# Filler products of two attentions moved to half as many places, two at a place

## The chip, the cores and the metric

One core of one Trainium2 chip runs the whole kernel. The metric is the device time of one launch in microseconds (us). Three runs of the kernel before took 2307.36, 2316.95 and 2318.63 us, median 2316.95 us. The profile is of one further execution.

## The reference, cut to what matters

The input is x of 8 sequences of 512 rows of 256 numbers. Each sequence goes through two blocks, both with 16 heads of 16 columns:

```python
x = x + layernorm(attention_1(layernorm(x)))      # causal, 250 keys back, rotary positions
x = x + layernorm(ffn(layernorm(x)))
# ffn(src):
sa  = attention_2(src)                            # full 512 x 512, rotary positions
x   = rmsnorm(src + sa)
shared = swiglu(x @ W_shared_in) @ W_shared_out   # 256 -> 2*512, then 512 -> 256
h      = swiglu(x @ W1_shared)                    # 256 -> 2*512
w      = gates of the best 2 of 8 experts in the better of 2 groups
routed = sum over e of (h @ W2_experts[e]) * w[:, e]   # 512 -> 256, eight times
out    = rmsnorm(x + shared + routed)
```

All experts are computed for all rows and weighted afterwards, so the amount of matrix work does not depend on the data.

## The kernel before, in words

Everything is computed transposed or straight as TensorE (PE) wants it, in tiles of 128 rows; a sequence is four such tiles. A pass of the outer loop (`batch`, eight passes) does both attentions of sequence i, and beside them the feed-forward part of sequence i-1, and the final norms of sequence i-2. Pass 0 has no feed-forward part to do; after the last pass the part of sequence 7 is done alone.

Each attention (`attention(i, f, e, a)`, a = 0 for the first and 1 for the second) is one list of steps, m from -28 to 63, and every engine walks the same list in its own order of instructions. There are 64 units (a head and a 128-row tile each, in four groups of four heads, 16 units to a group). At a step:

- `max_unit` (L644): for unit m+28, while there is one (that is for m up to 35), PE multiplies queries by keys into one of two PSUM banks (four banks for units 12 to 23). VectorE (DVE) takes the row maximum of it: L1008 with the mask for the first attention, L1011 for the second. The product for unit u waits until the maximum of unit u-2 (u-4 with four banks) has been taken.
- `score_unit` (L670): for unit m, from m = 0 on, PE computes the transposed scores with the maximum folded in; ScalarE (ACT) takes the exponential (L535), GpSimd (POOL) masks it in the first attention (L438, L442). The unit waits for the exponential of two units (later four units) before.
- `weigh` (L684): four times in a group PE multiplies four units' probabilities by the values; `max_rows` (L652) and `outputs` (L696) are four small transposes each, once in a group.
- Fillers: matrix products of the feed-forward part, which have nothing to do with this attention, stand at places given by two lists. `HIDDEN_AT` (32 entries, first attention) holds the up projections: entry s is one product of 128x128 by 128x512 in full fp32 (L710, `hidden`), which the trace shows as two instructions. Four entries make one block of hidden columns: two for the gated half into bank fb0, two for the other half into fb1. After the second of them ACT takes tanh (`ACT_LAG` = 1 step later), DVE the two elementwise products (`gated_half` and `hidden`, L1177 and L1184, `DVE_LAG` = 2 steps later); the next block's first product of a half waits for the DVE step that read that bank. `OUT_AT` (28 entries, second attention) holds the expert products: an entry is three products of 128x128 by 128x512 in fp32r (L732, `expert_out`), four entries make one output tile, which DVE adds to the sum with two instructions (L1199).

The order on PE within a step is: max unit, score unit, weigh and outputs where due, row transposes, then the filler. The two lists are worked out as

```python
QUIET = [g * UNITS + n for g in range(NGR) for n in (2, 5, 8, 12)]
QUIET_OUT = [g * UNITS + n for g in range(NGR) for n in (2, 8, 12)]
HIDDEN_AT = spread(8 * NH - len(QUIET), 10 - LEAD, -1) + QUIET
OUT_AT = spread(len(OUT_BESIDE) * NH - len(QUIET_OUT), 1 - LEAD, -1) + QUIET_OUT
```

With NGR = 4, UNITS = 16, NH = 4, LEAD = 28, the places of the up projections are -18 to -11, -9 to -3, -1, and then 2, 5, 8, 12, 18, 21, 24, 28, 34, 37, 40, 44, 50, 53, 56, 60. Those of the expert products are -27, -26, -24, -22, -21, -19, -17, -15, -14, -12, -10, -8, -7, -5, -3, -1, and then 2, 8, 12, 18, 24, 28, 34, 40, 44, 50, 56, 60.

The steps before m = 0 are called the lead below, those from 0 to 35 the body (max and score units), those from 36 on the tail (score units alone).

Of the kernel before, what the change touches and what calls it, by code (L numbers as in the profile page):

```python
# [22 lines left out]
NH = HID // P  # L23
# [5 lines left out]
NGR = H // GH  # L29
UNITS = GH * NT  # L30
# [5 lines left out]
LEAD = 28  # L36
# [3 lines left out]
def spread(steps, first, last):  # L40
    return [first + s * (last - first) // (steps - 1) for s in range(steps)]
# [2 lines left out]
LAST_STACKS_AT = 6 - LEAD  # L44
ROWS_FROM, LOGITS_AT = 2 - LEAD, 7 - LEAD

QUIET = [g * UNITS + n for g in range(NGR) for n in (2, 5, 8, 12)]
QUIET_OUT = [g * UNITS + n for g in range(NGR) for n in (2, 8, 12)]
HIDDEN_AT = spread(8 * NH - len(QUIET), 10 - LEAD, -1) + QUIET
OUT_FIRST, OUT_BESIDE = range(2, 7), range(9, 16)  # L50
OUT_END = {0: (((0, 0), (0, 1)), ((0, 2), (0, 3)), ((1, 0), (1, 1), (1, 2), (1, 3))),
           1: (((16, 0), (16, 1)), ((16, 2), (16, 3)), ())}
OUT_HEADS = {0: ((17,), (), (18,), (19,), ()), 1: ((), (7,), (), (8,), ())}
OUT_AT = spread(len(OUT_BESIDE) * NH - len(QUIET_OUT), 1 - LEAD, -1) + QUIET_OUT
ACT_LAG, DVE_LAG, HIGH_LAG = 1, 2, 3
GATES_FROM = LOGITS_AT + 2
GATE_EXPS_AT = (GATES_FROM + 6, GATES_FROM + 12)
# [11 lines left out]
def build(nc, x, in_w, out_w, wq, wkc, wvc, wk, wv, wo, w_si, w_so, w1, w2, wgg, weg,  # L69
# [3 lines left out]
    with ctx:  # L73
# [302 lines left out]
        def _(pool):  # L376
# [47 lines left out]
            def hidden_low(f, n):  # L424
                pool.wait_ge(s_hh, f * N_HH + n + 1)
                g.tensor_tensor(h_r[:, 1, n, :], sg[:, n % 2, :], h_r[:, 0, n, :].bitcast(F32),
                                ALU.subtract).then_inc(s_hl, 1)

            def mask_probs(i, f):

                for m in range(0, ALL, 2):
# [13 lines left out]
                    if f is not None:  # L445
                        for k in range(NH):
                            if min(HIDDEN_AT[4 * (NH + k) + 3] + HIGH_LAG, ALL - 1) // 2 * 2 == m:
                                hidden_low(f, k)
# [20 lines left out]
        def _(act):  # L469
# [37 lines left out]
            def tanh(f, n):  # L507
                act.wait_ge(s_up, f * N_UP + n + 1)
                if n >= 1:
                    act.wait_ge(s_sg, f * N_SG + n)  # L510
                nc.scalar.activation(th[:, :], fb[0][:, :], ACT.Tanh, scale=0.5).then_inc(s_th, 1)  # L511

            def hidden_high(f, n):
                act.wait_ge(s_ht, f * N_HT + n + 1)
                copy(h_r[:, 0, n - NH, :], sg[:, n % 2, :]).then_inc(s_hh, 1)
# [6 lines left out]
            def attention(i, f, a):  # L522
                for m in range(-LEAD, ALL):
# [15 lines left out]
                    if f is not None and a == 0:  # L539
# [4 lines left out]
                        for n in range(2 * NH):  # L544
                            if HIDDEN_AT[4 * n + 1] + ACT_LAG == m:
                                tanh(f, n)
                            if n >= NH and min(HIDDEN_AT[4 * n + 3] + HIGH_LAG, ALL - 1) == m:
                                hidden_high(f, n)
# [52 lines left out]
        def _(pe):  # L601
# [97 lines left out]
            def hidden(f, s):  # L699

                n, half, c = s // 4, s // 2 % 2, s % 2
                u, m = n // NH, n % NH
                if s == 0:
                    pe.wait_ge(s_gr, f + 1)
                elif n >= 1 and c == 0 and half == 0:
                    pe.wait_ge(s_sg, f * N_SG + n)
                elif n >= 1 and c == 0 and half == 1:
                    pe.wait_ge(s_ht, f * N_HT + n)
                col = half * HID + m * P
                product = mm(fb[half][:, :], wup_s[:, u, c, col:col + P], xn_t[:, c, :], start=(c == 0), stop=(c == NC - 1))  # L710
                if c == NC - 1:
                    product.then_inc((s_up, s_ub)[half], 1)

            def expert_out(f, q, m):

                k, t = divmod(q - NT, NT)
                rows = slice(t * P, (t + 1) * P)
                if m == 0:
                    if q == 0:
                        pe.wait_ge(s_ht, f * N_HT + 2 * NH)  # L720
                    if q == NT:
                        pe.wait_ge(s_hl, f * N_HL + NH)
                    if q >= 2:
                        pe.wait_ge(s_er, f * N_ER + q - 1)
                    if q >= NT and t == 0:
                        pe.wait_ge(s_w2[k % 2], f * N_W2 + 16 * (k // 2 + 1))
                if q < NT:
                    last = mm(fb[q % 2][:, 0:E], h_s[:, m, rows], wso_s[:, m, :], start=(m == 0), stop=(m == NH - 1))
                else:

                    for n, (h, w) in enumerate(((0, 0), (0, 1), (1, 0))):
                        last = mm(fb[q % 2][:, :], h_r[:, h, m, rows], w2_r[:, k % 2, w, m, :],  # L732
                                  start=(m == 0 and n == 0), stop=(m == NH - 1 and n == 2))
                if m == NH - 1:
                    last.then_inc(s_eo, 1)
# [18 lines left out]
            def attention(i, f, e, a):  # L754
                for m in range(-LEAD, ALL):
# [21 lines left out]
                    if f is not None and a == 0:  # L777
# [4 lines left out]
                        for s in range(8 * NH):  # L782
                            if HIDDEN_AT[s] == m:
                                hidden(f, s)
                    if f is not None and a == 1:
                        for s in range(len(OUT_AT)):
                            if OUT_AT[s] == m:
                                expert_out(f, OUT_BESIDE[s // NH], s % NH)
# [104 lines left out]
        def _(dve):  # L893
# [157 lines left out]
            def attention(i, f, e, a, more):  # L1051
# [9 lines left out]
                for m in range(-LEAD, ALL):  # L1061
# [8 lines left out]
                    if f is not None and a == 0:  # L1070
                        for n in range(2 * NH):
                            if HIDDEN_AT[4 * n + 1] + DVE_LAG == m:
                                gated_half(f, n)
                            if HIDDEN_AT[4 * n + 3] + DVE_LAG == m:
                                hidden(f, n)
                    if f is not None and a == 1:
                        for k, q in enumerate(OUT_BESIDE):
                            if OUT_AT[NH * k + NH - 1] + DVE_LAG == m:
                                expert_out(f, q)
# [91 lines left out]
            def gated_half(f, n):  # L1171
                dve.wait_ge(s_th, f * N_TH + n + 1)
                if NH + 2 <= n:
                    dve.wait_ge(s_hl, f * N_HL + n - 2 - NH + 1)
                elif n >= 2:
                    dve.wait_ge(s_ht, f * N_HT + n - 1)
                v.scalar_tensor_tensor(sg[:, n % 2, :], th[:, :], 1.0, fb[0][:, :], ALU.add,  # L1177
                                       ALU.mult).then_inc(s_sg, 1)

            def hidden(f, n):  # L1180
                dve.wait_ge(s_sg, f * N_SG + n + 1)
                dve.wait_ge(s_ub, f * N_UB + n + 1)
                block = h_s[:, n, :] if n < NH else sg[:, n % 2, :]
                v.scalar_tensor_tensor(block, sg[:, n % 2, :], 0.5, fb[1][:, :], ALU.mult, ALU.mult).then_inc(s_ht, 1)  # L1184
# [182 lines left out]
```

## Time and profile before

| | |
|---|---|
| median of three runs | 2316.95 us |
| the profiled execution's own time | 2316.51 us |
| its span, first to last instruction | 2314.5 us |
| PE busy | 2060.3 us, 89% |
| DVE busy | 1386.8 us, 60% |
| ACT busy | 829.0 us, 36% |
| POOL busy | 341.5 us, 15% |
| mean granted TensorE clock | 0.898 |

The profile is read by engine first, then by stage. A granted clock of 1.00 in a stretch means that TensorE ran at its upper level (2.4 GHz) all through it, 0.50 that it ran at the lower one (1.2 GHz). A stage below is named by its window in microseconds from the start of the span. Pass 2 has its first attention's body at 592.90 to 627.60 and its tail after it; pass 4 its second attention at 1260.40 to 1342.10.

### The profile page before, as it was taken

To read this page: it belongs to the slowest core of one execution; us is meant where nothing else is said; L and a number is where in the kernel's file an instruction comes from. 1 tells how busy PE (TensorE), PEld (TensorE's weight loads), DVE (VectorE), ACT (ScalarE), POOL (GpSimd) and SP (SyncE) were. 2 spreads that over 40 slices of the span, in tenths; PEclk is the share of its full clock that TensorE was granted. 3 is DMA by queue.
4 is the path that set the end of the run, shared out by engine and by line. 5 is a ranking of instruction groups with operands and counts; after the bars stand their busy time and mean duration, and the time that the engine had idled before them with its cause. 6 is when DMAs were issued, how large, how long until landed. Compare 5 with 4: busy or idle time off the path is not lost.

```text
span 2314.5 us, 31755 instructions
## 1 busy us (share of the span) xinstructions
PE 2060.3 (89%) x9200; PEld 1089.0 (47%) x9200; DVE 1386.8 (60%) x4293; ACT 829.0 (36%) x1713; POOL 341.5 (15%) x647
## 2 busy tenths in 40 slices
PE   6868899998999999999899989989899998999986
PEld 4343445535364453635436353453635545354455
DVE  6457455755756466674556756575565656747454
ACT  2434424262432424334242542325233262423410
POOL 3323112101220003100031011210112101210000
PEclk8577889998998988999789998898899899889988
DMA  4003002110030101101021010211002010020212
GB/s 166 2 28 138 1 2 92 37 38 10 6 133 1 48 1 73 66 2 48 1 83 55 7 42 1 90 49 38 11 2 101 37 38 10 6 89 35 77 52 91
DMA packets 23083, 104.64 MB, mean 45 GB/s; under 512 B 3312, under 2 KB 14192, under 8 KB 18288
## 3 DMA queue, kind: packets, MB, share of 16 engines
q1 hardware_dynamic: 21168, 89.81, 10.7%
q0 software_dynamic: 1728, 12.58, 1.4%
q8 instruction: 88, 1.44, 0.2%
q14 instruction: 99, 0.81, 0.1%
HBM read 84.56 MB, written 16.78 MB: 44 GB/s over the span
## 4 chain that ended last, share of the span: by engine, by line
PE 70%; DVE 19%; issue 7%; ACT 3%; DMA 0%; POOL 0%; DVEq 0%; SPq 0%; POOLq 0%; ACTq 0%
PE fb L732 13%; PE fb L710 11%; PE sm L644 10%; PE ot L684 10%; PE st L670 5%; PE st L629 3%; PE st L613 3%; DVE negmax L1011 2%; DVE acc L1199 2%; DVE stats L925 2%; PE dn L652 2%; PE dn L696 2%; PE dn L613 2%; PE sm L670 1%; DVE sm L1008 1%
## 5 line engine op out<-in xcount | busy, mean ns | idle before, releaser
L535 ACT ACTIVATE probs<-st 128x512 f32<-128x512 f32 (+3 forms) x832 | 404.9, 506 | 472.9 <-PE st L670 430.0
L644 PE MATMUL sm<-k_t,q_t 48*128 48x512 f32 (+3 forms) x928 | 381.0, 483 | 101.3 <-DVE negmax L1008 49.2
L732 PE MATMUL fb<-w_r,h_r 128*128 128x512 f32 x1536 | 444.3, 426 | 13.3 <-DVE acc L1199 13.3
L1011 DVE TENSOR_REDUCE negmax<-sm 128x1 f32<-128x512 f32 x464 | 302.7, 686 | 121.8 <-PE sm L644 120.3
L644 PEld LDWEIGHTS sm<-k_t,q_t 48*128 48x128 f32 x928 | 167.7, 207 | 435.8 <-DVE negmax L1008 211.9
L670 PE MATMUL st<-q_t,k_t 64*128 64x512 f32 (+3 forms) x832 | 352.0, 477 | 13.6 <-ACT probs L535 12.0
L732 PEld LDWEIGHTS fb<-w_r,h_r 128*128 128x128 f32 x1536 | 279.0, 195 | 126.0 <-issue 60.1
L710 PE MATMUL fb<-xn_t,wup_s 128*128 128x512 f32 x512 | 321.6, 723 | 6.8 <-DVE h_s L1184 4.1
L1008 DVE CUSTOM_DVE_ANT_0 sm<-sm,mask_qk 128x384 f32<-128x384 f32 (+2 forms) x464 | 213.3, 468 | 177.9 <-PE sm L644 175.4
L684 PE MATMUL ot<-probs,v_s 128*32 128x512 f32 (+3 forms) x2048 | 273.0, 554 | 3.2 <-POOL probs L438 1.8
L670 PEld LDWEIGHTS st<-q_t,k_t 64*128 64x128 f32 x832 | 153.0, 202 | 132.0 <-ACT probs L535 85.7
L399 POOL TENSOR_TENSOR stack<-rot,stack 128x256 fp32r<-128x256 f32 x64 | 47.8, 747 | 1131.2 <-ACT stack L471 1131.2
L438 POOL TENSOR_SCALAR_AFFINE_SELECT probs<-probs 128x256 f32<-128x256 f32 x256 | 107.7, 424 | 608.3 <-ACT probs L535 608.3
L1199 DVE SCALAR_TENSOR_TENSOR acc<-fb,gate,acc 128x256 f32<-128x256 f32 x256 | 123.4, 482 | 85.0 <-PE fb L732 78.2
L710 PEld LDWEIGHTS fb<-xn_t,wup_s 128*128 128x128 f32 x512 | 87.9, 210 | 65.6 <-issue 40.5
L629 PE MATMUL st<-ident,stack 128*128 128x128 f32 x704 | 109.1, 298 | 5.0 <-DVE q_t L997 3.9
L1028 DVE RECIPROCAL den<-dn 128x16 f32<-128x16 f32 x64 | 16.2, 253 | 156.1 <-PE dn L696 156.0
L511 ACT ACTIVATE th<-fb 128x512 f32<-128x512 f32 x64 | 38.1, 595 | 184.4 <-PE fb L710 184.4
L471 ACT ACTIVATE rot_b<-dn 8x512 f32<-8x512 f32 x64 | 36.8, 575 | 177.4 <-PE dn L652 177.4
L535 ACT ACTIVATE probs<-sm 128x512 f32<-128x512 f32 (+2 forms) x192 | 89.7, 493 | 20.9 <-PE sm L670 12.8
L629 PEld LDWEIGHTS st<-ident,stack 128*128 128x128 f32 x704 | 87.2, 153 | 18.0 <-issue 12.6
L471 ACT ACTIVATE stack<-rot 128x512 fp32r<-128x512 f32 x128 | 73.7, 625 | 49.9 <-DVE rot L992 48.7
(165 smaller groups left out, 2433.2 us busy)
## 6 DMA issues: line engine op xcount, KB each, us to landing
w_r<-w_parts SPq DMA_DIRECT2D x32, 2048.0 KB, 7.8
w_parts<-w_r POOLq DMA_DIRECT2D x4, 2048.0 KB, 8.8
x_s<-in_L_attn_query SPq DMA_DIRECT2D x8, 512.0 KB, 4.4
h_s<-in_L_ffn_W_experts POOLq DMA_DIRECT2D x8, 512.0 KB, 6.1
q_t<-rot_b SPq DMA_DIRECT2D x256, 4.0 KB
x_kept<-o_s SPq DMA_DIRECT2D x8, 512.0 KB, 3.1
xa<-x_kept SPq DMA_DIRECT2D x8, 512.0 KB, 3.9
out<-acc SPq DMA_DIRECT2D x8, 512.0 KB, 10.8
```

Source lines behind the costliest of these rows:

```text
L471: return nc.scalar.activation(dst, src, ACT.Copy)
L535: nc.scalar.activation(probs[:, n % PSLOTS, 0:hi - lo], score_bank(m)[:, 0:hi - lo], ACT.Exp, scale=float(D) ** -0.5).then_inc(s_ex, 1)
L613: last = mm(dst, src_t[:, c, t * P:(t + 1) * P], w[:, c, :], start=(c == 0), stop=(c == NC - 1))
L629: last = nc.tensor.transpose(stack_bank(a, t, k)[:, b * P:(b + 1) * P], stack[:, t % 2, pr:pr + 2, :].bitcast(F32).rearrange("p h s -> p ( ...
L644: mm(max_bank(w)[:, 0:hi - lo], q_t[r:r + MROW, b, t * P:(t + 1) * P], k_t[r:r + MROW, b, lo:hi], start=True, stop=True).then_inc(s_sm, 1)
L670: mm(score_bank(w)[:, 0:hi - lo], k_t[r:r + SK, b, j * P:(j + 1) * P], q_t[r:r + SK, b, lo:hi], start=True, stop=True).then_inc(s_st, 1)
L684: last = mm(ot[VW * c:VW * (c + 1), lo:hi], v_s[:, j, g * GH + c, :], probs[:, n % PSLOTS, 0:hi - lo], start=(j == 0), stop=(j == NT - 1), ...
L710: product = mm(fb[half][:, :], wup_s[:, u, c, col:col + P], xn_t[:, c, :], start=(c == 0), stop=(c == NC - 1))
L732: last = mm(fb[q % 2][:, :], h_r[:, h, m, rows], w2_r[:, k % 2, w, m, :], start=(m == 0 and n == 0), stop=(m == NH - 1 and n == 2))
L1008: return v.tensor_tensor_reduce(scores, scores, mask_qk[:, BACK * P - (hi - lo):BACK * P], -1.0, -MASKED, ALU.add, ALU.min, negmax[:, g % ...
L1011: return v.tensor_reduce(negmax[:, g % 2, n // GH, c:c + 1], max_bank(g * UNITS + n)[:, 0:hi - lo], AX.X, ALU.max, negate=True).then_inc(s ...
L1199: add = v.scalar_tensor_tensor(acc[:, t, :], fb[q % 2][:, (e % 2) * E:(e % 2 + 1) * E], gate[:, t, e:e + 1], acc[:, t, :], ALU.mult, ALU.add)
```

## The change

The lists hold every place twice, and half as many places. What stands at a place is then two up projections of the same half of a block, or two sets of three expert products of the same output tile. The amount of work, the order of the products among themselves and all the waits stay as they are.

```diff
-QUIET = [g * UNITS + n for g in range(NGR) for n in (2, 5, 8, 12)]
-QUIET_OUT = [g * UNITS + n for g in range(NGR) for n in (2, 8, 12)]
-HIDDEN_AT = spread(8 * NH - len(QUIET), 10 - LEAD, -1) + QUIET
+def doubled(places):
+    return [m for m in places for _ in range(2)]
+
+
+QUIET = [g * UNITS + n for g in range(NGR) for n in (4, 12)]
+QUIET_OUT = [g * UNITS + n for g, n in ((0, 4), (0, 12), (1, 4), (1, 12), (2, 12), (3, 4))]
+HIDDEN_AT = doubled(spread(4 * NH - len(QUIET), 10 - LEAD, -2) + QUIET)
 OUT_FIRST, OUT_BESIDE = range(2, 7), range(9, 16)
...
-OUT_AT = spread(len(OUT_BESIDE) * NH - len(QUIET_OUT), 1 - LEAD, -1) + QUIET_OUT
+OUT_AT = doubled(spread(len(OUT_BESIDE) * NH // 2 - len(QUIET_OUT), 1 - LEAD, -2) + QUIET_OUT)
```

The places of the up projections, two at each, are then -18, -16, -14, -12, -9, -7, -5, -2, and 4, 12, 20, 28, 36, 44, 52, 60. Those of the expert products, two sets at each, are -27, -24, -20, -17, -13, -10, -6, -2, and 4, 12, 20, 28, 44, 52.

## Rows read from the trace of the kernel before

**Rows 1.** The page: the clock in 40 slices (tenths), the chain by engine

```profile
PEclk8577889998998988999789998898899899889988
PE 70%; DVE 19%; issue 7%; ACT 3%; DMA 0%; POOL 0%; DVEq 0%; SPq 0%; POOLq 0%; ACTq 0%
```

**Rows 2.** Windows: start:end, us, busy PE, PEld, DVE, ACT, POOL, clock, DMA

```profile
574.50:592.90 18.40, 17.82 (x44) 6.21 (x42) 11.92 (x59) 2.48 (x5) 0.00 (x0) 1.00 0.01 1
592.90:627.60 34.70, 29.23 (x167) 11.56 (x167) 29.22 (x128) 17.83 (x43) 13.59 (x32) 1.00 0.01 3
627.60:647.50 19.90, 19.42 (x103) 7.53 (x101) 9.19 (x33) 12.02 (x31) 10.43 (x25) 1.00 0.57 214
1260.40:1285.70 25.30, 23.28 (x81) 11.79 (x81) 20.52 (x36) 0.59 (x1) 0.00 (x0) 1.00 0.00 1
1285.70:1321.60 35.90, 32.95 (x175) 13.39 (x174) 26.53 (x50) 21.89 (x40) 0.00 (x0) 1.00 0.01 2
1321.60:1342.10 20.50, 20.01 (x108) 7.37 (x107) 8.99 (x41) 15.42 (x30) 0.00 (x0) 1.00 0.29 104
```

**Rows 3.** Timeline of PE, first attention's lead, one product at a step

```profile
583.13 0.38 PE L644 MATMUL sm<-k_t,q_t 48*128 48x256 f32 x1
583.44 1.12 PE L710 MATMUL fb<-xn_t,wup_s 128*128 128x512 f32 x2
584.50 0.38 PE L644 MATMUL sm<-k_t,q_t 48*128 48x256 f32 x1
591.52 0.44 PE L644 MATMUL sm<-k_t,q_t 48*128 48x384 f32 x2
591.90 1.12 PE L710 MATMUL fb<-xn_t,wup_s 128*128 128x512 f32 x2
592.95 0.44 PE L644 MATMUL sm<-k_t,q_t 48*128 48x384 f32 x1
```

**Rows 4.** Chain of waits: products that follow each other (start, us)

```profile
2216.32 3.71 PE fb L710 x8
1252.99 2.81 PE fb L732 x12
```

**Rows 5.** Timeline of PE, pass 4: a product that waited for DVE

```profile
1131.80 1.12 PE L710 MATMUL fb<-xn_t,wup_s 128*128 128x512 f32 x2 [0.58 <-DVE h_s L1184]
```

**Rows 6.** Timeline, second attention's lead, PE and DVE

```profile
1266.26 0.49 PE L644 MATMUL sm<-k_t,q_t 48*128 48x512 f32 x1
1266.68 0.96 PE L732 MATMUL fb<-w_r,h_r 128*128 128x512 f32 x3
1266.79 0.69 DVE L1011 TENSOR_REDUCE negmax<-sm 128x1 f32<-128x512 f32 x1 [0.58 <-PE sm L644]
1267.57 0.50 PE L644 MATMUL sm<-k_t,q_t 48*128 48x512 f32 x2
```

**Rows 7.** Groups of DVE and waits in the window 592.9:627.6

```profile
L1008 DVE CUSTOM_DVE_ANT_0 sm<-sm,mask_qk 128x384 f32<-128x384 f32 x20 | 11.1, 556 | 2.6 <-PE sm L644 2.5
PEld sm L644 <- DVE negmax L1008: 19.3, 31, 1.0
```

**Rows 8.** Windows, first attention's body with tail, passes 4 and 7 of seven

```profile
1146.10:1209.80 63.70, 59.24 (x269) 22.27 (x268) 37.85 (x161) 29.89 (x74) 23.87 (x57) 0.79 0.19 68
1977.30:2046.00 68.70, 63.24 (x269) 23.42 (x268) 38.65 (x161) 30.02 (x74) 23.60 (x57) 0.75 0.19 71
```

**Rows 9.** Windows, the whole second attention, passes 4 and 6 of seven

```profile
1260.40:1342.10 81.70, 76.24 (x360) 32.54 (x360) 56.04 (x125) 37.90 (x70) 0.00 (x0) 1.00 0.08 27
1810.60:1900.60 90.00, 84.77 (x359) 35.89 (x359) 56.33 (x125) 37.53 (x70) 0.00 (x0) 0.87 0.07 25
```

**Rows 10.** Windows around a fall of the clock in pass 4, and a body

```profile
1145.90:1149.90 4.00, 3.01 (x13) 1.12 (x12) 3.90 (x15) 1.76 (x4) 0.78 (x2) 1.00 0.00 0
1149.90:1153.30 3.40, 3.22 (x8) 0.98 (x8) 2.48 (x15) 1.19 (x3) 1.58 (x4) 0.50 0.03 7
1146.10:1189.90 43.80, 39.83 (x168) 14.68 (x167) 28.74 (x128) 17.87 (x43) 13.43 (x32) 0.69 0.01 2
```

## The prediction

> **What bounds the kernel now.** I read the page's chain first, then the stages of one pass as windows, then the order of instructions inside a stage. The chain [rows 1] is 70% PE and 19% DVE: PE's stream sets the time, and DVE stops it here and there. The clock line [rows 1] dips below 9 in many slices, so a second question is how long PE runs at its lower level. The stages [rows 2] say where DVE counts. In the last part of the first attention's lead PE is busy 17.82 of 18.40 us and DVE 11.92: PE alone bounds it. In its body DVE is busy 29.22 of 34.70 and PE 29.23: the two hand over to each other, and PE's weight loads for max units waited 19.3 us on DVE's maxima [rows 7]. Its tail is PE's (19.42 of 19.90). In the second attention's lead DVE has 20.52 of 25.30 and PE 23.28, in the body PE 32.95 of 35.90, in the tail 20.01 of 20.50.
>
> What a filler costs is seen inside the lead. The max unit starts at 583.13, its product at 583.44, the next max at 584.50 [rows 3]: 0.31 us for a small matmul of 256 columns and 1.06 for the product, 1.37 a step. Two max units with no product between them start at 591.52, the product at 591.90, the next max at 592.95 [rows 3]: two of 384 columns took 0.38, hardly more than one. So a product between two max units costs its own time and also splits a pair that would have gone together. And products that follow each other take less than one alone: eight instructions, four products, took 3.71 us [rows 4], 0.93 each against 1.06.
>
> **The change part by part.** Seven passes (1 to 7) carry fillers; pass 0 and the part after the last pass have none of these places and stay as they are.
>
> 1. First attention's lead: 16 products at 16 steps become eight doubles. A double with the max before it, at the upper clock: 0.38 + 1.06 + 0.93 = 2.37 for 384 columns, where two steps were 2 x (592.95 - 591.52) = 2.86; with 256 columns 0.31 + 1.06 + 0.93 = 2.30 against 2.74 [rows 3, 4]. The mean is 0.46, eight doubles 3.7 us. One product waited 0.58 us for DVE's read of its bank [rows 5], once a lead; with doubles the read is due a step earlier against the bank's next use, and I take 0.4 of it. DVE's share of a double's two steps is two maxima and one elementwise product, about 11.92/18.40 of 2 x 1.4 us, 1.8 us, less than 2.3, so it does not become late. Together 4.1; I take 3.7, since the first two doubles run partly at the lower clock and one double straddles the row transposes. Seven passes: -26 us. Bounds per pass: -5 (0.6 more by the clock coming back one double earlier) and -2 (DVE late at every other double).
>
> 2. First attention's body and tail. Nine products stood in the body and seven in the tail, now eight and eight. In the body DVE has 5.5 us of slack in 34.7 [rows 2]. A single product of 1.06 behind two untaken maxima of 0.556 each [rows 7] is hidden for DVE; a double of 1.99 is not, and leaves it idle some 0.7 to 1.2 us, four times. Against it stands less PE time: 9 x 1.06 = 9.5 becomes 4 x 1.99 = 8.0, and five splits of 0.3 to 0.4 go, 1.7. I take -1.5 in the body. In the tail one product more: 7 x 1.06 = 7.4 becomes 8.0, less three splits, 1.1; but a weigh after a double must wait for exponentials and masks that could not start before it, where a single covered them. I take +0.5. Together -1 a pass, -7 us. Bounds: -4 and +3 a pass.
>
> 3. Second attention's lead: 16 sets become eight doubles. A step with a set takes 1.31 us (1266.26 to 1267.57), of which 0.42 is the max and 0.89 the set; DVE began the max 0.53 after PE did, having been idle 0.58 [rows 6]. A second set directly behind costs 3 x 2.81/12 = 0.70 [rows 4]. A double saves PE 0.19 and the split of 0.42. But DVE has 28 maxima of about 0.65 and four outputs of 1.0, over 22 of 25.3 us; where two banks are in turn it now idles 0.58 + 0.70 at a double, five times, where it idled 0.58 nine times, and where four banks are, nothing. That gives 6.4 against 5.2. I take 0, bounds -2 and +2 a pass.
>
> 4. Second attention's body and tail. Seven sets stood in the body and five in the tail, now eight and four. The body's PE time for them is 7 x 0.89 = 6.2 before and 4 x 1.59 = 6.4 after; three splits of 0.42 go, and DVE's idle at the doubles eats most of it: -0.5. The tail, PE's alone, loses 5 x 0.89 = 4.5 and gets 2 x 1.59 = 3.2, and two splits go: about -2, of which I take 1.2, because ACT's 28 exponentials become the next thing to be late (15.42 us busy in 20.5 [rows 2]). Together -1.7 a pass, -12 us. Bounds: -3 and +2 a pass.
>
> 5. The clock. In the seven first attentions body and tail together took 52.3, 54.6, 60.3, 63.7, 60.3, 54.6 and 68.7 us (two of the seven in [rows 8]); at the full clock it is 54.6, the body and tail of [rows 2]. The lower clock cost 35 us there. The seven second attentions took 81.4 to 90.0, together 28 us over seven times 81.7 ([rows 9] has the best full one and the worst). Before the fall in pass 4 PE had been busy 3.01 of 4.00 us, in steps 0 to 3, with one product only [rows 10]. After the change steps -1 to 3 hold no product, in each pass, nor do 13 to 19 and 29 to 35. So falls get likelier there: I take nine where there were four. But the double that follows keeps PE streaming for 4 us at the lower clock, so most are shorter; 5 us each, 45 for 35. In the second attention the thin places were in the lead, between single sets; doubles every three or four steps leave fewer, and I take half of the 28 away. Net -4; I count 0. Bounds: -28 (none left in the second attention) and +55 (six more passes at the price of pass 4's body, 43.80 against 34.70 [rows 2, 10], 9.1 each).
>
> The Trainium skill, page "TensorE: Matmul & The Clock Gate", section "A second HAM failure mode: psum-queue depth-cycling", says that short idles between groups of matmuls, coming often enough, make the clock swing between its two levels, and that what is lost is the time to warm up again. By it, fewer and larger groups with thinner stretches between them would speak against this change; it is the second rival below. The trace agrees at the one place quoted, and does not decide how often it comes.
>
> Nothing else moves. DVE's, ACT's and POOL's instructions keep their order and follow their products by the same lags; the POOL split of the hidden rows is due at the same steps 14, 28, 44 and 60, as each block's last entry still stands at 12, 28, 44 and 60. On SP's queue the expert weights' loads wait for output tiles that come at most two steps later or up to eight earlier, in a queue with nothing urgent behind it.
>
> The sum: -26 - 7 + 0 - 12 + 0 = -45; I shade the small terms, which are all differences between covers, by 3: -42. The profiled execution took 2316.5 us (span 2314.5 and 2.0 around it), the median of the runs 2316.95, so the two agree. 2316.5 - 42 = 2274.5, with the 0.45 between the two 2275.
>
> **The rivals.** (a) DVE becomes the bound beside the doubles: in the bodies it idles 1.2 us at four doubles where it idled 0.3 at nine or seven singles, +2.1 and +2.7 a pass, and in the second lead +1.1. Over seven passes +41, against part 1's -26: with half of the PE savings of parts 2 and 4 (-10 to -15), about 2318, no change. For it: the 19.3 us of waits [rows 7] and DVE's 29.22 of 34.70. Against it: fewer splits also mean fewer hand-overs. (b) The clock falls in the stretch before step 4 in all passes and stays low as in pass 4: part 1 stands, parts 2 to 4 give nothing, +55: 2316.5 - 26 + 55 = 2345, slower. It decides from about five more falls of that length, since 26 + 12 us must be made up. For it: one such fall in [rows 10] at a stretch with one product more than will stand there. Against it: the double's own 4 us. (c) More is gained: the lower clock vanishes from the second attention, -28 more, 2247.
>
> **How the numbers follow.** Forecast 0.55, (a) 0.18, (b) 0.15, (c) 0.12. About 0.5% of the time, 12 us, is what a measurement can tell from no change. The forecast's own range is 2250 to 2305; a few of its hundredths lie within 0.5%. Faster 0.64, same 0.20, slower 0.16. The range takes in (c) nearly whole and (a), and leaves (b) out: 2242 to 2322.
>
> **What would show it.** Part 1: the first attention's leads shorter by 3 to 4 us at equal clock, two max units starting together before each double, and four instructions of L710 in 2.0 us. Part 2: body at full clock near 33 us, tail near 20.5. Part 3: lead still near 25. Part 4: tail near 19. Part 5: windows at 0.50 at steps 0 to 8 of the first attention in most passes, but short, and fewer in the second. The prediction is wrong if the leads do not shrink, if DVE's idle in the bodies grows by more than 2 us a pass, or if the mean granted clock falls below about 0.87.

## The result and the profile after

| | before | after |
|---|---|---|
| median of 20 runs | 2326.77 us (2301.39 to 2338.92) | 2332.05 us (2320.56 to 2347.77) |
| ratio, 95% interval | | 1.0131 (1.0094 to 1.0167) |
| the profiled execution | 2316.5 us | 2338.5 us |
| its span, mean clock | 2314.5 us, 0.898 | 2336.5 us, 0.901 |

The change does not make the kernel faster. The ratio, taken from the fast executions of both alone, says 1.3% slower; the medians over all executions lie 0.2% apart. Where that difference comes from is part of the answer, and is settled below with the clock. The forecast was 2275.

The page of after, cut to the engines' busy time, the clock line and the chain by engine:

```profile
PE 2010.7 (86%) x9200; PEld 1106.0 (47%) x9200; DVE 1380.6 (59%) x4293; ACT 820.2 (35%) x1713; POOL 339.9 (15%) x647
PEclk8577999899899988999889998999899998899988
PE 67%; DVE 19%; issue 8%; ACT 4%; POOL 0%; DMA 0%; DVEq 0%; ACTq 0%; SPq 0%; POOLq 0%
```

PE is busy 2010.7 us, 49.6 less than before, in a span that is 22.0 longer. A saving of PE's busy time is there; PE's idle time grew by 71.6 us and took more than all of it. A pass has, by the stages below, 2.9 us more of this idle time in the first body, 3.1 in the second lead, 1.3 in the second body, 1.0 and 1.6 in the two tails, and only 0.3 in the first lead. The clock line holds 8 and 9 alone past its fourth slice, where before had a 7 in the middle [rows 1].

The stages, in windows with the columns of [rows 2]: pass 4's first attention (lead, body, tail), and pass 7's second attention (lead, body, tail):

```profile
1118.40:1153.20 34.80, 31.94 (x106) 17.44 (x106) 19.94 (x95) 5.57 (x11) 0.00 (x0) 0.80 0.00 1
1153.20:1190.50 37.30, 29.07 (x166) 12.51 (x163) 29.16 (x126) 17.61 (x43) 13.37 (x32) 0.94 0.01 2
1190.50:1216.10 25.60, 24.20 (x106) 9.47 (x103) 9.19 (x33) 11.29 (x31) 10.22 (x25) 0.83 0.50 186
2111.50:2138.00 26.50, 21.46 (x82) 12.18 (x82) 20.02 (x35) 0.59 (x1) 0.00 (x0) 1.00 0.00 1
2138.00:2177.30 39.30, 35.07 (x178) 14.91 (x175) 28.14 (x54) 21.80 (x40) 0.00 (x0) 0.96 0.01 2
2177.30:2200.20 22.90, 20.76 (x105) 7.54 (x104) 2.72 (x12) 14.93 (x30) 0.00 (x0) 0.93 0.47 169
```

The first lead has to be set against a lead of before with as much time at 1.2 GHz. Pass 2's whole lead of before has 13.7 us of it, as the first row above has:

```profile
554.30:592.90 38.60, 35.91 (x104) 16.73 (x104) 20.24 (x94) 5.67 (x11) 0.00 (x0) 0.82 0.00 1
```

38.6 against 34.8, -3.8 us: part 1 came as forecast. The second lead at the full clock is 26.5 us against 25.30 [rows 2]: PE is busy 1.82 us less in it and 1.2 us longer at it. Of the other stages most hold a short stretch at the lower clock, so they need its price. A body and a tail of before that differ in nothing else from those of [rows 2] give it. Windows of before, first attention of pass 3, body and tail:

```profile
868.00:904.10 36.10, 30.63 (x168) 12.09 (x167) 29.47 (x130) 17.83 (x43) 13.58 (x32) 0.95 0.01 2
904.10:928.30 24.20, 23.92 (x104) 8.79 (x101) 9.03 (x30) 12.02 (x31) 10.18 (x25) 0.79 0.53 195
```

The body has 3.3 us of the lower clock in it and takes 36.1 us beside the 34.7 of [rows 2], the tail 10.4 us of it and 24.2 beside the 19.9: 0.42 us lost for each us at 1.2 GHz.

With this price the 22 us between the two profiled executions part as follows (sums over passes 1 to 7, from the starts of max and score units; "low" is the change in time at 1.2 GHz, "work" is the length less 0.42 times low):

| stage | length | low | work | forecast |
|---|---|---|---|---|
| first lead | -29.0 | -10.9 | -24.4 | -26 |
| first body | +10.6 | +9.0 | +6.8 | -10.5 |
| first tail | +15.6 | +4.6 | +13.7 | +3.5 |
| second lead | +10.1 | +5.3 | +7.9 | 0 |
| second body | +9.1 | -19.1 | +17.1 | -3.5 |
| second tail | +15.3 | +20.4 | +6.7 | -8.4 |
| sum | +31.7 | +9.3 | +27.8 | -45 |

The price is one for all stages, and where it differs the split shifts: pass 4's first body lost 0.33 for each us (9.1 over 27.3 [rows 2, 10]), and in before's second bodies the 48.3 us of low clock cost only 14.8 (0.31 each), by which the second body's work is +12 instead of +17 and the sum +22. The rest, pass 0 and the joints between attentions, became 10 us shorter. Nothing was changed there except what the clock does. So the loss is one of work, 22 to 28 us, and it sits in five of the six stages.

### The profile page after: what moved, and what is told of

The parts are those of the page before. It is cut to its first block, busy times and chain, and to the rows that moved or that the text cites. A ratio compares the mean times of both kernels' runs of the same rounds, so it can differ in the third digit from the quotient of the medians.

```text
span 2336.5 us, 31755 instructions
## 1 busy us (share of the span) xinstructions
PE 2010.7 (86%) x9200; PEld 1106.0 (47%) x9200; DVE 1380.6 (59%) x4293; ACT 820.2 (35%) x1713; POOL 339.9 (15%) x647
## 3 DMA queue, kind: packets, MB, share of 16 engines
q1 hardware_dynamic: 21168, 89.81, 10.6%
## 4 chain that ended last, share of the span: by engine, by line
PE 67%; DVE 19%; issue 8%; ACT 4%; POOL 0%; DMA 0%; DVEq 0%; ACTq 0%; SPq 0%; POOLq 0%
PE fb L736 12%; PE fb L714 12%; PE ot L688 10%; PE sm L648 9%; PE st L674 4%; DVE negmax L1015 4%; PE st L633 3%; PE st L617 2%; PE dn L700 2%; DVE acc L1203 2%; DVE stats L929 2%; PE dn L656 1%; DVE sm L1012 1%; PE dn L617 1%; PE sm L674 1%
## 5 line engine op out<-in xcount | busy, mean ns | idle before, releaser
L648 PE MATMUL sm<-k_t,q_t 48*128 48x512 f32 (+3 forms) x928 | 356.1, 474 | 143.3 <-DVE negmax L1012 70.8
L736 PE MATMUL fb<-w_r,h_r 128*128 128x512 f32 x1536 | 422.7, 423 | 13.3 <-DVE acc L1203 13.3
L674 PE MATMUL st<-q_t,k_t 64*128 64x512 f32 (+3 forms) x832 | 330.3, 466 | 21.0 <-ACT probs L539 18.4
L648 PEld LDWEIGHTS sm<-k_t,q_t 48*128 48x128 f32 x928 | 155.5, 203 | 406.7 <-DVE negmax L1012 167.9
L736 PEld LDWEIGHTS fb<-w_r,h_r 128*128 128x128 f32 x1536 | 290.7, 197 | 112.8 <-issue 36.4
L714 PE MATMUL fb<-xn_t,wup_s 128*128 128x512 f32 x512 | 300.4, 721 | 2.5 <-DVE sg L1181 2.0
L688 PE MATMUL ot<-probs,v_s 128*32 128x512 f32 (+3 forms) x2048 | 281.3, 538 | 3.5 <-POOL probs L442 2.1
L674 PEld LDWEIGHTS st<-q_t,k_t 64*128 64x128 f32 x832 | 142.8, 198 | 132.8 <-ACT probs L539 66.3
L714 PEld LDWEIGHTS fb<-xn_t,wup_s 128*128 128x128 f32 x512 | 105.6, 227 | 108.3 <-issue 95.7
L475 ACT ACTIVATE rot_b<-dn 8x512 f32<-8x512 f32 x64 | 36.8, 575 | 181.3 <-PE dn L656 181.3
L688 PEld LDWEIGHTS ot<-probs,v_s 128*32 128x32 f32 x2048 | 53.8, 110 | 95.2 <-issue 43.6
```

Source lines behind the costliest of these rows:

```text
L475: return nc.scalar.activation(dst, src, ACT.Copy)
L648: mm(max_bank(w)[:, 0:hi - lo], q_t[r:r + MROW, b, t * P:(t + 1) * P], k_t[r:r + MROW, b, lo:hi], start=True, stop=True).then_inc(s_sm, 1)
L674: mm(score_bank(w)[:, 0:hi - lo], k_t[r:r + SK, b, j * P:(j + 1) * P], q_t[r:r + SK, b, lo:hi], start=True, stop=True).then_inc(s_st, 1)
L688: last = mm(ot[VW * c:VW * (c + 1), lo:hi], v_s[:, j, g * GH + c, :], probs[:, n % PSLOTS, 0:hi - lo], start=(j == 0), stop=(j == NT - 1), ...
```

## The experiments

**One list half at a time.** Each of the four kernels is before with one of the two lists doubled either in the lead or from step 0 on.

```diff
 # first lead alone
+HIDDEN_AT = doubled(spread(8, 10 - LEAD, -2)) + QUIET
 # first body and tail alone
+QUIET = doubled([g * UNITS + n for g in range(NGR) for n in (4, 12)])
 # second lead alone
+OUT_AT = doubled(spread(8, 1 - LEAD, -2)) + QUIET_OUT
 # second body and tail alone
+QUIET_OUT = doubled([g * UNITS + n for g, n in ((0, 4), (0, 12), (1, 4), (1, 12), (2, 12), (3, 4))])
```

> Doubles only in the first attention's lead; the other three stretches keep the single places of before. Theory S (the doubles save PE time everywhere, but away from the first lead they leave PE waiting for DVE and ACT): this part is the good one, -3.7 us a pass at equal clock, seven passes -26, ratio to before near 0.989; the second products end each double near 1.9 us. Rival Q (what made the whole change slower is the granted clock, falling in the stretches without a filler): this stretch has no such gap, so also about -26 here; the two part in the other three kernels.

> Doubles only in the first attention's body and tail. Theory S: in stretches at the full clock the body is 1 us longer and the tail 2 us longer than before, and the clock's falls at the two levels cost about what they cost before: +3 a pass, +20 in all, ratio 1.009; in the tail ACT idles over 1.5 us at each double. Rival Q: stages at the full clock are as long as before, and the extra comes only with windows at 0.50; then +0 to +10 us.

> Doubles only in the second attention's lead. Theory S: +1.2 us a pass at the full clock, since PE's busy time falls by 1.8 but its waits for DVE's maxima grow by 3: +8 us in all, ratio 1.004. Rival Q: no difference at the full clock (25.3 us), the lead longer only where the clock is low.

> Doubles only in the second attention's body and tail. Theory S: +2 us in the body and +1 in the tail at the full clock, +3 a pass, +20 in all, ratio 1.009. Rival Q: body 35.9 and tail 20.5 at the full clock as before, the rest by falls of the clock at step 4 and at step 38. If the four parts do not interact, the four differences add to the whole change's.

| doubled | median of 6 | ratio, 95% interval | mean clock |
|---|---|---|---|
| first lead | 2264.95 us | 0.9835 (0.9784 to 0.9886) | 0.909 |
| first body, tail | 2336.30 us | 1.0150 (1.0091 to 1.0210) | 0.899 |
| second lead | 2325.69 us | 1.0101 (1.0033 to 1.0170) | 0.898 |
| second body, tail | 2350.37 us | 1.0228 (1.0145 to 1.0310) | 0.891 |

Only the first of the four pays. **The kernel with the first lead doubled alone beats both kernels**, by 1.65% the one before. That is more than its lead saves: of the 62 us by which its mean lies under that of before's executions beside it, about half is clock (0.909 against 0.892), as is worked out below. By the ratios the parts add up to +3.1%, the whole change has +1.3%: they don't add. The stages do. Windows of the kernel with the first lead doubled (a lead with 13.7 us low), of the one with the first body and tail (a tail at the full clock), of the one with the second lead, and of the one with the second body and tail (its body has 3.4 us low, its tail none):

```profile
813.90:848.80 34.90, 32.01 (x105) 17.38 (x106) 19.95 (x95) 5.57 (x11) 0.00 (x0) 0.80 0.00 1
```
```profile
1482.30:1503.70 21.40, 20.01 (x106) 8.08 (x103) 9.39 (x34) 11.28 (x31) 10.19 (x25) 1.00 0.59 218
```
```profile
1836.70:1863.20 26.50, 21.47 (x82) 12.19 (x82) 20.04 (x35) 0.59 (x1) 0.00 (x0) 1.00 0.01 2
```
```profile
1291.20:1330.20 39.00, 35.16 (x177) 14.80 (x176) 27.89 (x54) 21.69 (x40) 0.00 (x0) 0.96 0.01 1
1330.20:1351.60 21.40, 19.27 (x105) 7.33 (x104) 7.68 (x36) 14.90 (x30) 0.00 (x0) 1.00 0.27 100
```

Against [rows 2], and for the first lead against the 38.6 above: first lead -3.7, first tail +1.5, second lead +1.2, second body +3.1 less 1.4 for the low clock, second tail +0.9. The same stages of the whole change have these lengths to within half a us, once the price of the lower clock is taken off. A rival, that stages at the full clock are as long as before and the clock alone costs the time, is out by these rows.

**What the executions' times say once the clock is taken out.** Each execution has a time and a mean granted clock. Before's 22 executions beside the experiments (one far off, 5611.69 us, left out) run from 2287.8 us at 0.912 to 2362.1 at 0.879: 74 us apart for one and the same program, and nearly all of it on a line. One line with a common slope through the executions below and six of a further kernel (four products at a place) is 19.4 us (within 1.5) for 0.01 of clock, and they scatter about it by 4 us. A hundredth of the clock is 46.6 us at 1.2 GHz in 2330, so this is 0.42 us for a us at the lower level again, from other data. Each kernel at a clock of 0.900:

| kernel | executions | mean clock | at 0.900 | against before |
|---|---|---|---|---|
| before | 22 | 0.891 | 2312.9 | |
| after | 20 | 0.904 | 2340.1 | +27.3, within 3.1 |
| first lead doubled | 6 | 0.909 | 2283.2 | -29.7, within 4.5 |
| first body, tail | 6 | 0.899 | 2335.8 | +22.9, within 3.8 |
| second lead | 6 | 0.898 | 2325.2 | +12.4, within 3.8 |
| second body, tail | 6 | 0.891 | 2334.8 | +21.9, within 3.6 |

The four parts now sum to +27.5, the whole change has +27.3, and the stages of one profile gave 22 to 28. So at an equal clock the parts add, and the structure of the schedule costs 27 us, 1.2%. The expectations had -26, +20, +8 and +20 for the four: the signs and the order are right. What does not add is the clock. After's executions have 0.012 more of it than these of before, worth 24 us. The clocks of before's 20 executions in the first table are, but for the profiled one, not on record; by the line their times stand for about 0.894, and the 0.010 from there to 0.904 is worth some 19 us, which leaves the few us between the medians. That the change itself raises the clock is likely and not shown: before has 0.890 to 0.892 on three chips, and the chip of after's 20 executions is not on record.

**Why doubles cost in bodies and tails.** Two pairs of kernels halve what DVE or ACT has to do and leave PE's work alone. In the first, the maxima are taken over the first half of the columns. In the second, the exponentials beyond the first few cover half of the columns, and the other half of the probabilities is what stood there, so that these kernels no longer compute the attention.

```diff
 # maxima, in take_max: over the first (hi - lo) // 2 columns
 # exponentials, in ACT's step for unit m
+w = hi - lo if m < PSLOTS else (hi - lo) // 2
```

> The kernel before, with DVE's row maxima taken over the first half of the columns only (the maximum is only an estimate then). It makes DVE's part of each unit shorter, 0.69 us to about 0.4 in the second attention. Base for the next kernel. Theory D (what doubles lose in the leads and bodies is PE waiting for DVE's maxima): second lead at the full clock from 25.3 down to some 23 us, since PE was waiting for DVE about 2 us of it. Rival: no change, 25.3.

> The changed kernel with the same halved maxima. Theory D: with DVE out of the way the sign turns: second lead 1 to 2 us shorter than that of the kernel before with halved maxima (it was 1.2 longer), second body at most as long as there (it was 1.7 longer). Rival E (the doubles lose by something of PE's own, or by ACT's exponentials): lead still +1.2, body still +1.7.

> The kernel before, with ACT's exponentials taken over half the columns from the ninth unit of each attention on (the other half of the probabilities is what was there). Base for the next kernel. Theory A (what doubles lose in the tails is PE waiting for exponentials after a double): tails at the full clock little changed here, 19.9 and 20.5 us to at best 19 and 19.5, since single places cover the waits.

> The changed kernel with the same halved exponentials. Theory A: the tails, 1.5 and 0.9 us longer at the full clock, become as short as or shorter than those of the kernel before with halved exponentials, in both attentions. Rival B (in the first attention it is POOL's masks and the copy of the weighed values that PE waits for): the second tail turns, the first stays 1 to 1.5 longer. Rival C (neither, the doubles' places are bad for PE itself): both stay.

Halved maxima: 2186.31 us with before's places and 2227.02 with after's, one execution each. Stages at the full clock, the kernel with before's places (second lead, second body) and then the one with after's (second lead, second body, first body, first tail):

```profile
666.50:689.80 23.30, 22.43 (x80) 11.39 (x80) 13.70 (x36) 0.59 (x1) 0.00 (x0) 1.00 0.01 2
689.80:724.30 34.50, 32.72 (x174) 13.44 (x173) 16.86 (x50) 21.68 (x40) 0.00 (x0) 1.00 0.01 2
```
```profile
675.10:698.10 23.00, 20.92 (x82) 12.11 (x82) 12.93 (x35) 0.59 (x1) 0.00 (x0) 1.00 0.01 2
698.10:734.90 36.80, 33.48 (x178) 14.04 (x175) 18.67 (x54) 21.57 (x40) 0.00 (x0) 1.00 0.01 2
833.10:865.60 32.50, 26.68 (x166) 11.34 (x163) 24.29 (x128) 17.52 (x43) 13.41 (x32) 1.00 0.01 3
865.60:887.10 21.50, 20.12 (x104) 8.23 (x104) 8.79 (x32) 11.28 (x31) 10.22 (x25) 1.00 0.59 219
```

The second lead turned from +1.2 to -0.3: there it was DVE. (The expectation had 1 to 2 us shorter, and a second body no longer than with single places.) The second body did not turn (34.5 to 36.8, +2.3), and the first body went from 31.9 to 32.5, the first tail from 19.7 to 21.5. In these, the columns of DVE's maxima are not the whole reason.

Halved exponentials: 2306.26 and 2316.97 us, one execution each. The second tail is 20.1 with either list, so its +0.9 went with the columns of ACT's exponentials. The first tail went from 19.4 to about 20.1 (22.0 with 4.5 us of the lower clock, less the price), +0.7 where it had been +1.5: half of it was ACT. The bodies kept about +0.9 (first) and +1.3 (second), by the same price.

The second tail with before's places, and the same with after's:

```profile
1587.80:1607.90 20.10, 19.63 (x107) 7.16 (x106) 9.03 (x41) 9.89 (x29) 0.00 (x0) 1.00 0.29 106
```
```profile
1600.10:1620.20 20.10, 18.43 (x105) 6.84 (x103) 7.98 (x39) 9.56 (x29) 0.00 (x0) 1.00 0.29 106
```

**Both halved.** Both edits in one kernel, with either list.

> The kernel before with both halvings, maxima and exponentials. Base for the next kernel. Bodies and tails at the full clock about as with the better of the two, 31.5 and 19.2 in the first attention, 33 and 20 in the second, as PE is then nearly alone the bound.

> The changed kernel with both halvings. Theory W (with either engine alone made quicker PE still waits for the other after a double; what doubles lose in bodies and tails is the sum of both kinds of waits): body and tail together at the full clock no longer than those of the kernel before with both halvings, in the second attention, where they were +2.6 with none, +3.2 with the maxima halved and +1.3 with the exponentials halved; in the first at most +1, for POOL's masks. Rival R (order on PE itself): +2 or more stays in both.

2178.36 us with before's places and 2193.61 with after's. Second attention's body and tail, before's places and then after's:

```profile
680.70:713.80 33.10, 31.69 (x174) 13.04 (x173) 16.84 (x49) 15.94 (x40) 0.00 (x0) 1.00 0.01 2
713.80:733.90 20.10, 19.63 (x108) 7.16 (x106) 8.82 (x41) 9.90 (x30) 0.00 (x0) 1.00 0.29 106
```
```profile
1214.50:1249.40 34.90, 32.93 (x179) 14.08 (x176) 18.59 (x54) 15.78 (x40) 0.00 (x0) 1.00 0.01 2
1249.40:1269.50 20.10, 18.43 (x105) 6.84 (x104) 7.67 (x36) 9.56 (x29) 0.00 (x0) 1.00 0.29 106
```

PE's busy time over both stages is 51.32 and 51.37 us: the same sets, and nothing saved by having fewer splits. The body is 1.8 us longer, 1.24 of it busy time (the set that came to it from the tail, 0.89 [rows 6], and 0.35 besides) and 0.6 idle. The tail has 1.20 us less to do and is no shorter, with ACT busy only 9.56 us and DVE 7.67. The first attention keeps +0.7 in the body and +0.5 in the tail. So a loss of 1.2 us a pass in the first attention and 1.8 in the second is left, where the expectation had at most 1 and none. PE's waits name where it sits. The first attention's bodies (1078.0:1110.2 of the kernel with before's places, 1342.5:1375.4 of the one with after's), then the second's bodies in the windows above:

```profile
PE sm L645 <- DVE negmax L1010: 2.5, 6, 0.6
PE sm L649 <- DVE negmax L1014: 5.1, 10, 1.0
PE sm L645 <- DVE negmax L1013: 0.8, 3, 0.3
PE sm L649 <- DVE negmax L1017: 1.5, 4, 0.7
```

The second attention's tail, one row with before's places and two with after's:

```profile
PE st L671 <- ACT probs L536: 0.5, 1, 0.5
PE st L675 <- ACT probs L540: 0.9, 2, 0.5
PE dn L701 <- ACT o_t L475: 0.7, 1, 0.7
```

In the bodies PE still waits longer for DVE, halved as the maxima are. In the tail there is a wait that neither halving touches: the transposes of the outputs (`dn`) stand for ACT's copy of the weighed values (`o_t`), 0.7 us, and do so in the first attention's tail too. No run takes these waits away one by one, so what each of them costs is read from the traces and not tested.

**Four products at a place.** In the first lead the doubles paid, so fours might pay more.

```diff
+HIDDEN_AT = doubled(doubled(spread(4, 10 - LEAD, -3))) + QUIET
```

> The first attention's lead with four products at each of four places (-18, -14, -9, -3 or so), everything else as before. Theory P (in this lead PE alone is the bound, and each group of products less saves one small matmul's split, 0.3, and 0.1 between products): four groups less than with doubles, about 0.4 each, another -1.5 us a pass, lead near 28 at the full clock, ratio to before near 0.980. Rival D (a group of four, 3.8 us, starves DVE, whose maxima then come late): as long as with doubles or 1 us longer, ratio 0.984 to 0.99.

2359.80 us (2344.88 to 2374.74), ratio 1.0150 (1.0074 to 1.0226); at an equal clock +11.4 us (within 3.9) against before, where doubles have -29.7. A lead of it, with 20.5 us at the lower clock:

```profile
836.60:878.60 42.00, 34.80 (x105) 18.95 (x105) 19.68 (x95) 5.67 (x11) 0.00 (x0) 0.76 0.00 1
```

PE idles 7.2 of 42.0 us in that lead, where it idled 2.9 of 34.8 with doubles and 2.7 of 38.6 with singles: a four takes 3.7 us [rows 4], DVE takes the two maxima that it has meanwhile and idles (5.8 us behind one four at the lower clock), and then PE waits for it, 6.1 us in the lead where it waited 2.8 with doubles. Another 1.1 us are waits of a four's first product for DVE's read of its bank. The mean clock fell to 0.881 as well. Both theories were off: one had the lead 1.5 us a pass shorter than with doubles, the other at most 1 us longer, and at an equal clock it is about 4 us longer. Of one, two and four at a place two is the best in this lead.

**The double at step 4 split.** The clock falls before step 4 in five of seven passes of the first attention. Here one of its two products goes to step 1, in both lists.

```diff
+HIDDEN_AT[HIDDEN_AT.index(4)] = 1
+OUT_AT[OUT_AT.index(4)] = 1
```

> The changed kernel with one of the two at step 4 moved to step 1, in both attentions. Theory C (the clock falls there because steps -1 to 3 hold no product): the windows of 0.50 just before or at step 4 go or get rare in both attentions, while those at steps 20, 36 and 52 of the first attention stay; bodies 1 to 2 us shorter. Rival: the fall has to do with something else at the body's start, and comes at the same step.

2320.39 us in one execution, at 0.904; at that clock after has 2332.3 by the line above, so some 12 us less, as far as one execution tells. The first attention's bodies and tails had 65 us less of the lower clock than in the profile of after, the second's leads and bodies 38 more. The theory held by half. In the first attention no fall is left before step 4; but those at steps 20, 36 and 52, where nothing was changed and which it expected to stay, went from 18 to 7. In the second attention four of seven passes have a stretch of 13.7 us at the lower clock from about step -3 to step 7, although step 1 now holds a set. So an empty stretch is not all that decides on a fall, and one execution does not tell what else does. The trace has both bodies at the full clock, of the first attention (pass 6) and of the second, which shows the work of this kernel's bodies without any correction:

```profile
1709.70:1744.90 35.20, 27.31 (x166) 11.35 (x163) 28.79 (x126) 17.57 (x43) 13.40 (x32) 1.00 0.01 3
1843.40:1880.70 37.30, 33.91 (x178) 14.03 (x175) 28.13 (x54) 21.80 (x40) 0.00 (x0) 1.00 0.01 2
```

## Why the prediction was wrong

**The views that it was built on were right**, and so was part 1: forecast -26, measured -24.4 in the stages and -29.7 at an equal clock. The lead was PE's alone [rows 2], its doubles start as the forecast drew them, a pair of max units and then 1.98 us of products, and PE's idle time in it grew by only 0.3 us a pass.

**Part 2 failed, and it is the first of two large errors: -7 forecast, +20.5 measured.** The step that failed is "five splits of 0.3 to 0.4 go, 1.7", and in the tail "less three splits, 1.1". That saving was read from the lead, where PE hardly waits. In a body PE's weight loads wait for DVE at most steps (31 times, 19.3 us in all [rows 7], much of it behind products that still run), and PE itself stands idle 5.5 of 34.7 us. The full-clock body above, of the kernel with the step 4 double split, has PE's busy time 1.92 us lower (29.23 [rows 2] to 27.31). The ninth product, now in the tail, is 1.06 of that, so that fewer splits and products directly behind others gave 0.86 between them. PE's idle time grew by 2.4 us, and the body became longer by 0.5. Nearly all of the 2.4 is one wait, before and then with the double split:

```profile
PE sm L644 <- DVE negmax L1008: 4.0, 7, 0.8
PE sm L650 <- DVE negmax L1014: 6.1, 10, 0.8
```

The forecast's own terms warned of it: 1.5 us of products and 1.7 of splits saved, against an idle of "0.7 to 1.2 us, four times", 2.8 to 4.8, do not come to the -1.5 that it took. A reading that fits the rows, argued and not tested by itself: a single product covered DVE's or ACT's time; two together cover one such time with twice the work and leave the next bare. In the tail the splits failed again: at the full clock PE is busy 20.01 us in the kernel with this part alone, and 19.42 before, so the added product counts with its 0.6 and the "three splits, 1.1" are not there. The danger that the forecast named ("a weigh after a double must wait for exponentials and masks") stood in its +0.5 with about 1 us, and PE's idle time did grow by 0.9. Timeline of after, first tail of pass 2, behind the double at step 52:

```profile
646.94 0.49 ACT L539 ACTIVATE probs<-st 128x384 f32<-128x384 f32 x1 [3.38 <-PE st L674]
647.59 0.41 POOL L442 TENSOR_SCALAR_AFFINE_SELECT probs<-probs 128x256 f32<-128x256 f32 x1 [3.48 <-ACT probs L539]
648.35 0.18 PEld L674 LDWEIGHTS sm<-q_t,k_t 64*128 64x128 f32 x1 [0.38 <-ACT probs L539]
649.67 0.14 PEld L688 LDWEIGHTS ot<-probs,v_s 128*32 128x32 f32 x4 [0.49 <-POOL probs L446]
650.45 0.18 PEld L674 LDWEIGHTS st<-q_t,k_t 64*128 64x128 f32 x1 [0.63 <-ACT probs L539]
```

The number in brackets is the idle time before the row, and who ended it. ACT stands idle 3.38 us (here at the lower clock) while the two products run, since no score unit comes between them; then its exponentials and POOL's masks are late for the next three things that PE's weight loads want. At the full clock these hardly stop PE itself. In the tail of the kernel with this part alone the idle time that was added is one other wait, the outputs' transposes (`dn`) for ACT's copy of the weighed values:

```profile
PE dn L700 <- ACT o_t L475: 0.9, 1, 0.9
```

**Part 3: 0 forecast, +7.9 measured, within its bound of 2 a pass.** The step that failed is the saving of PE, 0.19 and "the split of 0.42" at each of eight doubles, 4.9 us: at the full clock PE's busy time fell by 1.82 (23.28 to 21.46), 0.23 a double, so that next to nothing came of the splits. PE's idle time grew from 2.0 to 5.0. The sum "6.4 against 5.2" of DVE's idle gives +1.2, and the lead is +1.2 longer; that the two figures are equal is luck, since all of DVE's idle in the window went from 4.8 to 6.5 us. Waits of after in the second lead of pass 7, and under them one of before in the same stage:

```profile
DVE negmax L1015 <- PE sm L648: 5.3, 6, 1.3
PE sm L648 <- DVE negmax L1015: 3.7, 5, 1.2
```
```profile
PE sm L644 <- DVE negmax L1011: 1.9, 2, 1.0
```

DVE waits up to 1.3 us at a double, and then PE waits up to 1.2 us for DVE (3.7 us in all, 1.9 in before). With the maxima halved this wait of PE is 1.5 us in the same stage with doubles and 0.9 with singles, and the doubles come out 0.3 us ahead.

**Part 4, the other large error: -12 forecast, +18 to +24 measured.** Three steps of it failed. The splits were again no saving (PE's 51.32 and 51.37 us above). The set that moved from tail to body cost its full 0.9 in the body: PE's busy time is 0.96 up there (32.95 to 33.91), which is most of the body's +1.4. And in the tail "about -2, of which I take 1.2, because ACT's 28 exponentials become the next thing to be late" had the right engine and both sizes wrong: PE's busy time fell by 0.74 (20.01 to 19.27 in the kernel with this part alone), and its idle time grew by 1.64, 0.7 for exponentials and 0.9 for ACT's copy of the weighed values. The tail of [rows 2] had fillers at five places with scores between; of its last 11 steps none has one now. In the body DVE idles 1 us behind a double, as rival (a) had it, but in sum it idles no longer than before (9.2 us in the 37.3 of the kernel with the step 4 double split, 9.4 in the 35.9 of [rows 2]). Timeline of the kernel with the step 4 double split, second body of pass 6, full clock:

```profile
1854.78 1.29 DVE L1017 TENSOR_REDUCE negmax<-sm 128x1 f32<-128x512 f32 x2 [1.01 <-PE sm L650]
1854.91 1.66 PE L738 MATMUL fb<-w_r,h_r 128*128 128x512 f32 x6
1856.50 0.18 PEld L650 LDWEIGHTS sm<-k_t,q_t 48*128 48x128 f32 x1 [0.37 <-DVE negmax L1017]
1857.04 1.29 DVE L1017 TENSOR_REDUCE negmax<-sm 128x1 f32<-128x512 f32 x2 [0.97 <-PE sm L650]
1857.07 1.09 ACT L541 ACTIVATE probs<-st 128x512 f32<-128x512 f32 x2 [1.17 <-PE st L676]
```

**Part 5: 0 forecast, +4 measured in the six stages, and a gain elsewhere.** Each step of it was off. It took nine falls for four in the first attentions; there are 23, before step 4 in five passes, at 20 in six, at 36 in all seven, at 52 in five. It said most would be short, and they are: in passes 2 to 7 none in an attention's body or tail is longer than 6.8 us without a break (pass 1 has one of 13.7 around the start of its second body), where before had 27.3 in pass 4 and 34.1 in pass 7. In the second attention they did not halve; the low time went from 82 to 88 us. They come at fixed places. The same 9 us of passes 4 and 5, around step 36, of after:

```profile
1188.00:1197.00 9.00, 7.89 (x25) 3.53 (x24) 5.02 (x24) 3.54 (x9) 3.06 (x6) 0.62 0.00 0
1468.00:1477.00 9.00, 8.01 (x26) 3.67 (x30) 4.89 (x21) 3.53 (x9) 3.14 (x7) 0.62 0.00 0
```

The places in the first attention are the ends of the stretches without a filler. The section of the Trainium skill that the prediction named ("TensorE: Matmul & The Clock Gate", "A second HAM failure mode: psum-queue depth-cycling") says that the clock swings between its levels where short idles come often enough, and it does here. The many short swings cost no more than the few long falls that they replace, by the executions: 0.904 on average against 0.891.

**The rivals.** (a) named the mechanism for the second lead and part of the first body. Its +41 a kernel lies near the measured +47 to +52 outside the first lead, but partly by luck: it counts DVE's idle time in two bodies and a lead, of which the second body has no more than before, and leaves out the tails, which have 20 of the measured us. (b) had the sign right and the reason wrong: its falls came, and did not stay. The range ended at 2322, since the savings of parts 2 to 4 had been read in the leads and used in stages with other limits. None of the prediction's signs of being wrong came: the first leads shrank, DVE's idle time in the two bodies grew by 1.4 us a pass together, the mean clock stayed near 0.90. They watched DVE and the clock, and the loss was in PE's idle time.

## What to carry to other kernels

A filler between dependent steps is worth what it covers, not what it costs its engine. Where the engine hardly waits (here the first lead, 97% busy in its last part), fill coarsely and save the splits; where it waits for others again and again, keep one small filler in each wait. Price a regrouping stage by stage, never with a saving read in a stage of another limit, and before believing a difference of 1% put the executions of both kernels on one line against the mean granted clock.

## What the runs showed of the hardware

How the clock falls differs from one execution to the next of the same program, and that is nearly all of the spread of the times: before varies by 74 us over 22 executions, after by 27 over 20, the kernel with the first lead alone by 10 over six.

The maxima over half of the columns, with before's places, took 2186.31 us where before took 2332.20 beside it on the same chip: 146 us, where the doubles moved 30. By the line some 91 of it is the clock, which rose from 0.890 to 0.937 (no fall was left in a body, a tail or a second lead of passes 1 to 7), and 55 is work; the line is drawn out there beyond the clocks that it was fitted to, 0.876 to 0.912, so the split is an estimate. That is one execution of a smaller computation. It says that DVE's maxima cost this kernel more than their time: the waits that they cause also come with the lower clock.
